# Attention scores of four heads per group, in four row tiles of TensorE and four PSUM banks

## What is computed

```python
x = _layernorm(x + _L0_attn_ref(x, ...))      # RWKV-like mixing along the 16 steps
x = _layernorm(x + _L0_xattn_ref(x, ctx_768, Wq, bq, Wk, bk, Wv, bv, Wo, bo))
x = _layernorm(x + _L0_ffn_ref(x, w_gate, w1_e, w3_e, w2_e, w1_s, w3_s, w2_s))
```

```python
attn = jnp.einsum('bhqd,bhkd->bhqk', q, k) * scale     # scores: 256 x 256 for each head
attn = jnp.clip(attn, -CLAMP, CLAMP)
attn = jax.nn.softmax(attn, axis=-1)
x = jnp.einsum('bhqk,bhkd->bqhd', attn, v).reshape(B, Nq, Cq)
return x @ Wo + bo
```

## Time and profile before

| | |
|---|---|
| median of three runs | 1237.92 us |
| the profiled execution | 1229.94 us |
| its span, first to last instruction | 1228.1 us |
| TensorE busy | 1075.5 us (88%), mean granted clock 0.945 |
| VectorE busy | 842.4 us (69%) |
| ScalarE busy | 662.9 us (54%) |
| GpSimd busy | 573.2 us (47%) |

### The profile page before, as it was taken

One profiled execution on the slowest core, in us unless ns is written; L12 is line 12 of the kernel. 1 busy time (PEld: TensorE's weight loads), 2 busy tenths in 40 slices (PEclk: granted clock), 3 DMA queues, 4 the chain that ended last, 5 costly groups with the idle time before them and its releaser, 6 DMA issues.

```text
span 1228.1 us, 21376 instructions
## 1 busy us (share of the span) xinstructions
PE 1075.5 (88%) x6580; PEld 815.5 (66%) x6580; DVE 842.4 (69%) x1706; ACT 662.9 (54%) x1924; POOL 573.2 (47%) x567
## 2 busy tenths in 40 slices
PE   4789999999999999999879999999989885877771
PEld 2566666767767677667657777877767774666650
DVE  2456889788898898898968566565544422554758
ACT  0365676666756756666536666657664342433210
POOL 5633644746548448457343533511111125544765
PEclk9888999989999999999879999999999897988995
DMA  9512224224133221011222232122223554666543
GB/s 263 160 49 70 72 83 144 98 78 136 56 127 104 68 97 50 35 50 51 94 76 75 79 105 93 62 95 78 91 87 113 163 162 139 185 195 191 156 128 120
DMA packets 106429, 131.27 MB, mean 107 GB/s; under 512 B 10176, under 2 KB 94032, under 8 KB 106320
## 3 DMA queue, kind: packets, MB, share of 16 engines
q1 hardware_dynamic: 94800, 98.43, 25.2%
q0 software_dynamic: 11520, 31.47, 8.2%
HBM read 60.66 MB, written 69.21 MB: 106 GB/s over the span
## 4 chain that ended last, share of the span: by engine, by line
PE 62%; DVE 19%; issue 6%; another core or an unknown queue 5%; ACT 4%; POOL 2%; DMA 1%; SPq 1%; DVEq 0%; ACTq 0%; POOLq 0%
PE bT L531 8%; PE bS L704 8%; PE bY L754 7%; PE bM L517 6%; PE bO L725 3%; DVE Sc L1186 3%; PE bU L634 3%; PE bS L789 3%; PE bC L738 3%; DVE nmx L1188 3%; PE bM L565 2%; PE bC L791 2%; PE bU L661 2%; PE bM L524 2%
## 5 line engine op out<-in xcount | busy, mean ns | idle before, releaser
L965 ACT ACTIVATE Sc<-Sc,nmx 128x256 f32<-128x256 f32 x512 | 252.8, 500 | 0.0
L1186 DVE TENSOR_SCALAR Sc<-bS 128x1024 f32<-128x1024 f32 x128 | 155.1, 1212 | 135.4 <-PE bS L704 129.9
L973 ACT ACTIVATE PT<-bT 128x512 f32<-128x512 f32 x256 | 151.4, 591 | 172.5 <-PE bT L531 163.8
L1607 POOL DMA_INDIRECT yg<-Ys,yslots x120 | 117.1, 976 | 135.6 <-DVE acc L1426 56.2
L531 PE MATMUL bT<-idn,Sc 128*128 128x128 f32 x1024 | 168.2, 288 | 10.5 <-ACT PT L973 9.9
L531 PEld LDWEIGHTS bT<-idn,Sc 128*128 128x128 f32 x1024 | 115.1, 144 | 85.6 <-issue 54.9
L1583 POOL DMA_INDIRECT Xs<-x,slots x120 | 118.9, 990 | 109.3 <-DVE slots L1280 77.9
L1533 POOL TENSOR_TENSOR rstd<-vpe,mhalf 128x2 f32<-128x2 f32 x48 | 35.0, 733 | 272.9 <-DVE vpe L1111 272.3
L1188 DVE TENSOR_REDUCE nmx<-Sc 128x4 f32<-128x1024 f32 x128 | 156.2, 1220 | 4.4
L704 PE MATMUL bS<-KT,QT 32*128 32x256 f32 x1024 | 150.6, 412 | 1.9 <-DVE Sc L1186 1.9
L704 PEld LDWEIGHTS bS<-KT,QT 32*128 32x128 f32 x1024 | 90.4, 190 | 40.1 <-issue 30.3
(11 more groups left out here) (198 smaller groups left out, 2040.0 us busy)
## 6 DMA issues: line engine op xcount, KB each, us to landing
Xs<-Wo SPq DMA_DIRECT2D x16, 1408.0 KB, 7.4
xb<-Xs SPq DMA_DIRECT2D x152, 128.0 KB
Ys<-yb SPq DMA_DIRECT2D x76, 256.0 KB
W<-w SPq DMA_DIRECT2D x4, 1152.0 KB, 11.1
xTs<-xT SPq DMA_DIRECT2D x16, 256.0 KB
x<-x SPq DMA_DIRECT2D x16, 256.0 KB, 4.0
Base<-stg SPq DMA_DIRECT2D x15, 256.0 KB
acc<-Base SPq DMA_DIRECT2D x15, 256.0 KB
```

The lines of the kernel that those rows point to most:

```text
L965: last = fn(Sc[:, n % 3, m, t, :], Sc[:, n % 3, m, t, :], ACT.Exp, bias=nmx[:, n % 3, m, t:t + 1], accum_out=rs[:, s % 2, t, h:h + 1])
L973: fn(flat(PT[:, h % RING]), bT[:, :], ACT.Copy).then_inc(a_pt.sem, 1)
L1186: ts(Sc[:, n % 3].rearrange("p m t k -> p (m t k)"), flat(bS[:, :, :]), CLAMP, -CLAMP, ALU.min, ALU.max).then_inc(d_clip.sem, 1)
L1607: pool.indirect_dma_start(yg[:, j % AHEAD, k, :], None, Ys[e.k], bass.IndirectOffsetOnAxis(ap=yslots[:, l, q:q + 1], axis=0)).then_inc(s_y ...
```

## The change

Slots up to START, 94 of the 128 pairs, get their scores for two pairs at once. In an even slot TensorE makes the scores of pairs n+2 and n+3: for each t four matmuls in the four row tiles 0, 32, 64 and 96, which write four banks. In an odd slot it makes none. The four banks are one tensor `four`; the first two are `bS`, the other two are `bC` and `bY`, which the routed experts use only later. VectorE's clip takes the even pair from `bS` and the odd one from the other two (`score_banks`). One signal at the end of the eight matmuls counts for two. `turn_rows(0)`, the first to write `bC`, waits for the clip of pair 93. All other programs stay as they are, and so do VectorE's and ScalarE's orders.

```diff
@@ -89,6 +89,7 @@
 
 
 START = slot_of(11, 6)
+QUADS = START - slot_of(0, 0)
 TAIL = slot_of(L, 0)
 AHEAD, LATE, BASES, XBUFS = 4, 3, 5, 3
 
@@ -236,13 +237,20 @@
         dig = spare.rearrange("p (q e) -> p q e", e=E)
 
 
-        bS = ctx.enter_context(nc.psum_tensor("bS", [P, 2, 512], F32))
-        bU, bC, bY, bT, bO, bM = (bank(n) for n in ("bU", "bC", "bY", "bT", "bO", "bM"))
+        four = ctx.enter_context(nc.psum_tensor("four", [P, 4, 512], F32))
+        bS, bC, bY = four[:, 0:2], four[:, 2], four[:, 3]
+        bU, bT, bO, bM = (bank(n) for n in ("bU", "bT", "bO", "bM"))
 
         def cols(b, n=2):
             return b[:, :].rearrange("p (n c) -> p n c", n=n)
 
-        cut = bS[:, :, :].rearrange("p m (t k) -> p m t k", t=NT)
+        def score_banks(n):
+
+            return four[:, 2:4] if n < QUADS and n % 2 else bS
+
+        def cut(n):
+
+            return score_banks(n).rearrange("p m (t k) -> p m t k", t=NT)
 
 
         s_att = sem("s_att")
@@ -689,20 +697,26 @@
                     last = pe.transpose(bM[0:1, n * P:(n + 1) * P], bcol[:, n:n + 1], idn[:, :])
                 last.then_inc(p_cols.sem, 1)
 
+            def score(n, m, t):
+                s, g = divmod(n, HEADS // 2)
+                r, j, odd = HB * (2 * (g % 2) + m), g // 4, g // 2 % 2
+                return mm(cut(n)[:, m, t, :], QT[r:r + HB, s % 2, odd, j, t * P:(t + 1) * P], KT[r:r + HB, s % 2, j, :], start=True, stop=True)
+
             def scores(n):
 
                 s, g = divmod(n, HEADS // 2)
+                if n < QUADS and g % 2:
+                    return
                 if g == 0:
                     pe.wait_ge(a_k.sem, a_k.at(s))
                     pe.wait_ge(a_q.sem, a_q.at(s))
                 if n:
                     pe.wait_ge(d_clip.sem, d_clip.at(n - 1))
-                j, odd = g // 4, g // 2 % 2
                 for t in range(NT):
-                    for m in range(2):
-                        r = HB * (2 * (g % 2) + m)
-                        last = mm(cut[:, m, t, :], QT[r:r + HB, s % 2, odd, j, t * P:(t + 1) * P], KT[r:r + HB, s % 2, j, :], start=True, stop=True)
-                last.then_inc(p_s.sem, 1)
+                    for k in (n, n + 1) if n < QUADS else (n,):
+                        for m in range(2):
+                            last = score(k, m, t)
+                last.then_inc(p_s.sem, 2 if n < QUADS else 1)
 
             def turn_probs(n, m):
                 h = 2 * n + m
@@ -728,6 +742,8 @@
 
             def turn_rows(i):
                 pe.wait_ge(s_xb[i % XBUFS], 32 * (i // XBUFS + 1))
+                if i == 0:
+                    pe.wait_ge(d_clip.sem, d_clip.at(QUADS - 1))
                 if i:
                     pe.wait_ge(a_xb.sem, a_xb.at(i - 1))
                 if i >= 2 and not late(i - 2):
@@ -1183,7 +1199,7 @@
                 dve.wait_ge(p_s.sem, p_s.at(n))
                 if n >= 3:
                     dve.wait_ge(p_t.sem, p_t.at(2 * n - 5))
-                ts(Sc[:, n % 3].rearrange("p m t k -> p (m t k)"), flat(bS[:, :, :]), CLAMP, -CLAMP, ALU.min, ALU.max).then_inc(d_clip.sem, 1)
+                ts(Sc[:, n % 3].rearrange("p m t k -> p (m t k)"), flat(score_banks(n)), CLAMP, -CLAMP, ALU.min, ALU.max).then_inc(d_clip.sem, 1)
                 dve.wait_ge(d_clip.sem, d_clip.at(n))
                 dve.tensor_reduce(flat(nmx[:, n % 3]), Sc[:, n % 3].rearrange("p m t k -> p (m t) k"), AX.X, ALU.max, negate=True).then_inc(d_max.sem, 1)
 
```

## The result

The changed kernel took 1258.29 us (median of four runs, 1253.84 to 1264.66) beside 1236.19 for the kernel before (four runs, 1229.12 to 1243.02): 1.018 times as long, with a 95% interval of 1.011 to 1.026. In a second comparison it was 1.021 (1.017 to 1.025). The forecast was 1256. The profiled execution took 1253.84 us, its span is 1252.0, 23.9 more than before.

What follows compares the result with a forecast made beforehand. TensorE was nearly full, but the chain of waits also ran through VectorE and ScalarE. Profiled 1229.94 - 2.1 direct gain - 4.8 replaced falls + 30.2 new clock falls + 3.2 long falls = 1256 us; range 1226 to 1272.

Steps and rivals of the forecast that it cites:

- one pair plus 0.01 us: Price of a double group of eight score matmuls on TensorE, against 1.13 us for one pair's scores.
- The bound of two pairs one behind the other: Upper bound for a double group, 1.06 + 1.13 us; as a rival (tiles not four abreast) chance 0.12.
- Slots 1, 3 and 7 gave nothing: TensorE already waits behind these slots' scores for ScalarE or VectorE, so dropping the scores gains 0 there.
- Slot 5's pause: Slot 5's turn waits for ScalarE's copy: gain 0.14 us per step, new TensorE pause of about 0.9 us.
- 0.14 - 4 x 0.01 = 0.10: Direct gain per step: slot 5's 0.14 us less 0.01 us for each of four double groups on the chain.
- steps of 47.5 us: Sign of the forecast: attention step length wherever TensorE's clock stays at 1.00.
- one pause of 2.40: Slot 3, where TensorE waits for the x2 VectorE normalises: its 1.34 us pause grows to 2.40 us.
- 1.8 falls per step: TensorE clock falls behind longer pauses: 0.8 at slot 3, 0.5 each at slots 1 and 7, 1.60 us each.
- two of nineteen at three times: Two of nineteen clock falls last three times as long, adding 2 x 1.6 = 3.2 us.
- 30.2 + 3.2 = 33.4 us: Cost of TensorE clock falls over ten and a half steps: 30.2 us, plus 3.2 us for long ones.
- clock as before: Rival: longer pauses stay harmless to TensorE's clock, leaving only the direct gain; 1228 us, up to 1240; chance 0.20.
- The VectorE rival: VectorE as only bound: steps shrink by its waits for scores, 1.06 to 3.5 us; 1219 to 1193 us; chance 0.08.

Runs made afterwards that it cites:

- fill_all: Changed kernel with unneeded matmuls in three pauses: ahead of slot 1's first turn, the turn of x2 and the second shared matmul; 1162.55 us, 0.989 times the kernel before.
- refill: Changed kernel with the even pair's scores made once more in each odd slot, read by nobody; 1167.22 us, 0.996 times the kernel before.
- half_scores: Kernel before with the scores of odd pairs below pair 94 left out, output wrong; 1216.46 us, 1.038 times the kernel before.
- early_five: Changed kernel with double groups and context values moved into pauses, and slot 5's projections and shared matmul ahead of its turns; 1216.24 us, 0.981 times the kernel before.
- fill_slot3: Changed kernel with three unneeded matmuls only ahead of the turn of x2 in slot 3; 1256.68 us, 1.014 times the kernel before.
- fill_slots_1_7: Changed kernel with unneeded matmuls only ahead of slot 1's first turn and the second shared matmul; 1165.55 us, 0.993 times the kernel before.
- after_again: Changed kernel run once more, unaltered, in a later group of runs; 1264.76 us, 1.021 times the kernel before.
- before_fill: Kernel before with two unneeded matmuls in its own 1.34 us pause ahead of the turn of x2; 1176.64 us, 1.002 times the kernel before.
- five_again: early_five run once more, unaltered, in the last group of runs; 1148.71 us, 0.981 times the kernel before.

## Why the prediction was right

- *The price of a double group.* 1.15 us in place of 1.13, with the next group 1.08 instead of 1.06 us behind: the 0.01 of "one pair plus 0.01 us" was 0.02. The bound of two pairs one behind the other was far off: the four row tiles run abreast.
- *What reaches the end.* Slots 1, 3 and 7 gave nothing, as said. Slot 5's pause was 0.88 (about 0.9), and the turn there waits for ScalarE's copy. From the scores of slot 4 to those of slot 6 it takes 438.75 - 427.01 = 11.74 us at full clock (before 11.87). `fill_all` measures the whole of it, 0.07 us per step, where the sum has 0.14 - 4 x 0.01 = 0.10 and steps of 47.5 us were named as a sign (47.63 came).
- *The pauses.* Slot 1: 1.46, as forecast. Slot 7: 1.57 instead of 1.38. Slot 3: not one pause of 2.40 but 0.44 ahead of the context keys and 1.88 ahead of x2; I had added 1.06 to the last wait without looking at what stands before it, and the context keys wait for VectorE too.
- *How often the clock falls.* 1.8 falls per step were forecast, 15 in nine steps (1.67) came. The split was off: 0.8, 0.5 and 0.5 for slots 3, 1 and 7 against 0.67, 0.67 and 0.33. Two fifths of the falls lasted twice as long, where I had two of nineteen at three times: nine steps at 47.63 would be 428.7 us, so fifteen falls cost 461.1 - 428.7 = 32.4 us, 2.2 each instead of 1.6 to 1.8. The forecast had 30.2 + 3.2 = 33.4 us for ten and a half steps, which is 28.6 for nine.
- *Luck in the total.* For the nine steps the sum has 28.6 - 0.9 - 4.8 = 22.9 us more than before, and 27.0 came. For all the rest it has 3.6 us more, and 3.1 less came, mainly because the start is 6.2 us shorter, with its 10 us fall replaced by a short one, for which the sum has no term. These two misses, 4 and 7 us, go opposite ways, and so 26.5 us of forecast growth stand beside 23.9 measured. The mechanism was right; that the total came within 3 us was luck in part.
- *Cause.* `refill`, `half_scores` and `fill_all` show it from three sides: without the pauses no loss, with the pauses alone more loss, with the pauses filled a kernel faster than before. The last one shows what the "clock as before" case would have been: had the clock held, the change would have been worth its 0.07 us per step.
- *The VectorE rival.* Its 3.5 us per step of waits could be had in part, but not by this change: in an undisturbed step of `early_five` they are 1.41 + 0.27 = 1.7 us, and the step is 1.7 us shorter (47.70 to 46.00).
- *What the sum had wrong.* Slot 3 as the main place: `fill_slot3` changes nothing in the nine steps, `fill_slots_1_7` gives back nearly all of them. I ranked the pauses by length, and length alone doesn't rank them. Why the same 1.88 us pause is followed by a fall in six of nine steps of the changed kernel and in one of nine of `fill_slots_1_7` stays open.

## What to carry to other kernels

Before work is taken off the busiest engine, follow the chain of waits place by place: TensorE was busy for 95% of a step, and of 4.2 us freed per step 0.07 reached the end. Freed TensorE time that becomes pauses can cost more clock than it saves, here above all in the two pauses next to small matmuls; move useful work into the pauses (here the next double group and an independent projection), and fill what is left. A saving that is worth next to nothing in one order can be worth much in another: the same double groups gave 0.07 us per undisturbed step at first and 1.45 in the order of `early_five`.

## What I had not expected

- Unneeded matmuls in its pauses made the changed kernel 1.1% faster than the one before (`fill_all`) and its runs steadier: 6 us between the fastest and the slowest of ten, against 17 us in 19 runs.
- In `fill_slot3` the steps settled at 51.2 us each, with two falls in each, and in its first profile the changed kernel repeats every three steps (50.4, 52.4, 50.8 us; in `after_again` it does so for three steps only). There removing one pause moved the falls instead of thinning them out. Why they fall into such patterns is open.
- The kernel before took 1236 to 1243 us in two groups and 1172 to 1173 us in the two others. Undisturbed inner steps take 47.70 us in both kinds (`before_fill` for the others). The difference is in the part behind them: from the clip of pair 88 to the end it takes 655.1 us in the kernel before and 597.1 in `refill`. There GpSimd's gathers wait for VectorE's sums 56.2 us in all in the first profile, and 6.9 us in `refill` (waits of GpSimd from 900 us on, of the kernel before and of `refill`):

```profile
POOL yg L1607 <- DVE acc L1426: 56.2, 14, 7.2
```

```profile
POOL yg L1634 <- DVE acc L1453: 6.9, 7, 1.7
```

`after_again`, in the group at 1243, has 58.1 us of this wait, `five_again`, in the one at 1172, 6.1. These groups ran on different chips; what makes them differ there is open; every ratio is taken within one group.
